# Stage boundaries of a two-layer audio tower: scatters awaited by the next stage's loads, row additions on another engine, a value table made in pieces

## The reference, cut to what matters

```python
h = signature_tokens(x) @ W.T + b                    # (32, 255, 128)
h = h + fuzzy_attention(layernorm(h))                # layer 0
h = h + experts_top1(layernorm(h))                   # 8 experts, hidden 512
h = h + relative_attention(layernorm(h))             # layer 1, 8 heads, tables of relative positions
h = h + experts_top2(layernorm(h)) + shared(...)     # 64 experts, 256 places each, hidden 64
```

## Time and profile before

| | us |
|---|---|
| median of 3 runs (lowest to highest) | 2033.37 (2031.94 to 2037.08) |
| the profiled execution, its own time | 2041.06 |
| its span in the trace | 2039.2 |
| busy in it: PE | 1724.1 |
| DVE | 1439.4 |
| ACT | 928.7 |
| POOL | 854.7 |

### The profile page before, as it was taken

How to read it: one execution, slowest core, us unless ns; L and a number is a source line. 1 busy time by engine, 2 the same in 40 slices (tenths; PEclk the granted TensorE clock), 3 DMA queues, 4 the chain that set the end, 5 groups by cost and what they waited for, 6 DMA issues and landing times. The chain is left out here.

```text
span 2039.2 us, 59053 instructions
## 1 busy us (share of the span) xinstructions
PE 1724.1 (85%) x21927; PEld 1418.4 (70%) x21927; DVE 1439.4 (71%) x3457; ACT 928.7 (46%) x2320; POOL 854.7 (42%) x1705
## 2 busy tenths in 40 slices
PE   4999999999979964994799999999999999857740
PEld 3888888888757754993577777777777777634420
DVE  6777777777668864666877888888888888644323
ACT  2211111112166722773566667666676667414320
POOL 2333333333103654666211333444444444447770
PEclk9999999999988966997799999999999999879775
DMA  8900000000040002223233333333333333345537
GB/s 300 137 0 0 0 0 0 0 0 0 1 176 11 25 28 57 71 71 109 46 62 60 70 75 70 74 70 77 73 79 74 73 73 78 86 115 158 153 94 253
DMA packets 312955, 147.80 MB, mean 72 GB/s; under 512 B 205142, under 2 KB 291572, under 8 KB 312308
## 3 DMA queue, kind: packets, MB, share of 16 engines
q1 hardware_dynamic: 300164, 118.58, 25.1%
q0 software_dynamic: 12544, 25.91, 3.9%
HBM read 72.23 MB, written 73.37 MB: 71 GB/s over the span
## 5 line engine op out<-in xcount | busy, mean ns | idle before, releaser
L1943 ACT ACTIVATE rel_e<-rel_s_ps,rel_neg_max 128x255 f32<-128x255 f32 x512 | 199.9, 478 | 42.0 <-DVE rel_neg_max L2262 41.3
L2262 DVE TENSOR_REDUCE rel_neg_max<-rel_s_ps 128x4 f32<-128x1020 f32 x128 | 156.2, 1220 | 88.4 <-PE rel_s_ps L1684 85.6
L524 PE MATMUL tok_main_ps<-tok_w_h,tok_feat_h 128*128 128x512 f32 x512 | 204.4, 399 | 1.1 <-DVE tok_feat_low L99 1.1
L524 PE MATMUL tok_main_ps<-tok_w_h,tok_feat_l 128*128 128x512 f32 x512 | 199.9, 390 | 0.0
L524 PE MATMUL tok_main_ps<-tok_w_l,tok_feat_h 128*128 128x512 f32 x512 | 199.7, 390 | 0.0
L84 POOL TENSOR_TENSOR tok_q_pre<-tok_v_q,tok_v 128x128 f32 (+1 forms) x32 | 38.8, 1213 | 305.8 <-DVE tok_q L273 291.5
L1668 PE MATMUL rel_s_ps<-rel_k_h,rel_q_head_h 128*128 128x256 f32 x512 | 156.0, 305 | 0.2 <-DVE rel_q_head_l L2233 0.2
L1705 PEld LDWEIGHTS rel_t_ps<-all_k_ident,rel_e 128*128 128x128 f32 x1024 | 109.6, 140 | 65.6 <-issue 64.5
L1705 PE MATMUL rel_t_ps<-all_k_ident,rel_e 128*128 128x128 f32 x1024 | 138.9, 278 | 11.9 <-issue 11.7
L2130 POOL DMA_INDIRECT x_slots<-rel_x,rel_at x128 | 129.9, 1015 | 38.8 <-issue 34.0
L1668 PE MATMUL rel_s_ps<-rel_k_h,rel_q_head_l 128*128 128x256 f32 x512 | 145.4, 284 | 0.0
(11 more groups left out here) (402 smaller groups left out, 4677.3 us busy)
## 6 DMA issues: line engine op xcount, KB each, us to landing
rel_q_rep<-q_rows SPq DMA_DIRECT2D x256, 64.0 KB
o_rows<-rel_rv SPq DMA_DIRECT2D x256, 64.0 KB
x_slots<-early_zeros SPq DMA_DIRECT2D x16, 520.0 KB, 6.2
exp_x<-x_slots SPq DMA_DIRECT2D x32, 260.0 KB, 3.0
y_rows<-early_zeros SPq DMA_DIRECT2D x16, 512.0 KB, 5.9
final_y<-y_rows SPq DMA_DIRECT2D x16, 512.0 KB, 10.8
exp_x<-x_slots SPq DMA_DIRECT2D x72, 65.0 KB, 1.9
q_rows<-rel_qT SPq DMA_DIRECT2D x64, 64.0 KB
```

The lines of the kernel that those rows point to most:

```text
L524: nc.tensor.matmul(main_ps[s][:, cols], feat[fk][:, s, j, :], w_p[wk][:, j, cols], start=(j == 0 and (fk, wk) == (0, 0)), stop=False)
L1943: last = nc.scalar.activation(e[u % 2][:, n, 0:L], s_ps[u % 2][:, n, 0:L], ACT.Exp, bias=neg_max[u % 2][:, n:n + 1])
L2262: nc.vector.tensor_reduce(neg_max[u % 2][:], s_ps[u % 2][:, :, 0:L], AX.X, ALU.max, negate=True)\
```

## The change

Four things are changed.

1. **Waits moved.** The semaphores of the scatters and of the padding are allocated in `build` and outlive their stages. The waits at the end of POOL's and SP's programs are gone. SP waits for the same counts in the next stage, in front of its first load: 5 semaphores and `padded` in `experts_top1`, 8 in `relative_attention`, 3 in `experts_top2`, 8 in `add_pairs`. The DRAIN and both barriers stay.
2. **Table in pieces.** In `experts_top1` DVE makes the table in 16 pieces of [128, 16 x 16], one at the end of each of steps 8 to 23, and the bias in step 24, in place of two instructions after step 71.
3. **Row additions on DVE.** DVE adds all eight chunks. Chunks 1 and 2 come behind `read_x(0)`, 3 and 4 in the head, 5, 6 and 7 in slots 1, 2 and 3 of sequence 0. Statistics: chunk 1 in the head, 2 to 5 in slots 0 to 3 of sequence 0, 6 and 7 in slots 0 and 1 of sequence 1. POOL makes the factors in two parts, chunks 1 to 3 and then 4 to 7. ACT waits for five additions ahead of the slots and for all eight in its first `rows`; DVE no longer waits. `eT` is allocated in front of `q_rep`.
4. **Order of the first loads of `experts_top2`.** SP first issues the matrices of three pairs of experts, then waits for the scatters, then loads the rows of these three, the shared matrices and the shared rows, then the rest.

```diff
@@ fuzzy_attention
-                sp.wait_ge(padded, 16 * E0)
...
-                for n in range(NB):
-                    pool.wait_ge(sent[n], 16 * CT * len(range(n, N, NB)))
@@ experts_top1
+                for j in range(NB0):
+                    sp.wait_ge(slots_sent[j], 16 * 2 * G * len(range(j, NT // (2 * G), NB0)))
+                sp.wait_ge(padded, 16 * E0)
                 for j in range(U):
                     load(j, j)
...
-                for j in range(U):
-                    pool.wait_ge(y_out[j], 16 * (ST0 // U))
...
-                def attention_tables():
-
-                    attention.wait(dve)
...
-                    for t, lo in ((1, 0), (0, 2 * P)):
-                        nc.vector.tensor_tensor(vtab[:, lo:lo + P, :], vtab[:, lo:lo + P, :],
-                                                ends[:, t:t + 1, :].to_broadcast([P, P, HD]), ALU.subtract)\
+                PIECE = 16
+                FIRST = 8
+
+                def attention_tables(n):
+
...
+                    if n == 0:
+                        attention.wait(dve)
+                        nc.vector.tensor_scalar(bq[:], bq[:], 1.0 / float(D) ** 0.5, None, ALU.mult)
+                    if 0 <= n < 2 * (P // PIECE):
+                        t, lo = ((1, 0), (0, 2 * P))[n // (P // PIECE)]
+                        rows = slice(lo + n % (P // PIECE) * PIECE, lo + (n % (P // PIECE) + 1) * PIECE)
+                        nc.vector.tensor_tensor(vtab[:, rows, :], vtab[:, rows, :],
+                                                vends[:, t:t + 1, 0:HD].to_broadcast([P, PIECE, HD]), ALU.subtract)\
                             .then_inc(table_ready, 1)
...
+                def with_tables(i, j):
+                    step(i, j)
+                    attention_tables(U * i + j - FIRST)
+
                 loaded.wait(dve)
-                run(step, 3)
-                attention_tables()
+                run(with_tables, 3)
@@ relative_attention
+                for j in range(U0):
+                    sp.wait_ge(y0_out[j], 16 * (ST0 // U0))
                 for c in range(NCH):
...
+                    if b == 0:
+                        act.wait_ge(rows_added, NCH)
...
-                    act.wait_ge(rows_added, NCH - 1)
+                    act.wait_ge(rows_added, 5)
...
-                for c in range(1, NCH):
-                    pool.wait_ge(y_in[c], 16)
-                    hc = h[:, c * CH:(c + 1) * CH, :]
-                    nc.gpsimd.tensor_tensor(hc, hc, y_at[c], ALU.add).then_inc(rows_added, 1)
-
-                def norm_rest():
+                def norm_rest(lo, hi):
...
+                    pool.wait_ge(rows_stats, hi // CH)
...
-                norm_rest()
+                norm_rest(CH, MID)
+                norm_rest(MID, NT)
...
-                for n in range(NX1):
-                    pool.wait_ge(sent[n], SENT1 * len(range(n, NC1, NX1)))
...
+                def add_rows(c):
+                    hc = h[:, c * CH:(c + 1) * CH, :]
+                    dve.wait_ge(y_in[c], 16)
+                    nc.vector.tensor_tensor(hc, hc, y_at[c], ALU.add).then_inc(rows_added, 1)
...
+                    if 2 * b == MID:
+                        dve.wait_ge(norm_ready, 2)
...
-                    if b == 0 and u in (1, 2):
-                        stats_of_rows(NCH - 3 + u)
+                    if b == 0 and u >= 1:
+                        add_rows(4 + u)
+                    if b == 0:
+                        stats_of_rows(2 + u)
+                    if b == 1 and u < 2:
+                        stats_of_rows(6 + u)
...
                     read_x(0)
-                    stats_of_rows(1)
-                    stats_of_rows(2)
+                    add_rows(1)
+                    add_rows(2)
                     keys_remainder(0, 0)
                     read_x(1)
-                    stats_of_rows(3)
+                    stats_of_rows(1)
                     read_v(0, 0)
                     queries_remainder(0, 0, range(4))
                     keys_remainder(1, 1)
-                    stats_of_rows(4)
+                    add_rows(3)
                     position_queries(0, 0)
-                    stats_of_rows(5)
+                    add_rows(4)
                     maxima(0, 0)
                     queries_remainder(1, 1, (0,))
                     read_x(2)
-                    dve.wait_ge(rows_added, NCH - 1)
@@ experts_top2
-                for j in range(U):
-                    load(0, j)
-                    if j == 1:
-                        for to, src in ((sw1_sb, sw1), (sw3_sb, sw3), (sw2_sb, sw2)):
-                            sp.dma_start(to[:], src).then_inc(sw_in, 16)
+                AHEAD = 3
+                for j in range(AHEAD):
+                    load_weights(0, j)
+                for j in range(NX1):
+                    sp.wait_ge(slots1_sent[j], 16 * CT1 * TOPK1 * len(range(j, NC1, NX1)))
+                for j in range(AHEAD):
+                    load_x(0, j)
+                for to, src in ((sw1_sb, sw1), (sw3_sb, sw3), (sw2_sb, sw2)):
+                    sp.dma_start(to[:], src).then_inc(sw_in, 16)
+                load_shared(0, 0)
+                for j in range(AHEAD, U):
+                    load_x(0, j)
+                    load_weights(0, j)
...
-                for j in range(U):
-                    pool.wait_ge(y_out[j], SENT * (N // U))
@@ add_pairs
+                for j in range(U1):
+                    sp.wait_ge(y1_out[j], 16 * (2 * CAP // P) * (E1N // 2 // U1))
                 for c in range(N):
```

More of the change, by code:

```diff
@@ L677, with fuzzy_attention @@
 CLEARS1 = (SLOTS1 + TOPK1 * NT * P) // (AGAIN * PER * P)
-def fuzzy_attention(nc, K, h, mean, rstd, stats, weights, x_slots, no_token, tables, cleared, behind):
+def fuzzy_attention(nc, K, h, mean, rstd, stats, weights, x_slots, no_token, tables, cleared, behind, sent, padded):
     ident = K["ident"]
@@ L1178, in experts_top1 @@
         x_in = [m.sem(f"x_in{j}") for j in range(U)]
-        y_out = [m.sem(f"y_out{j}") for j in range(U)]
         turned, xT_ready, w1_ready, w2_ready, hid_done, hid_a, hid_v, y_done, y_ready, tick_ready = (
@@ L1410, with relative_attention @@
 SG = 8
[L1413 removed]
+def relative_attention(nc, K, h, mean, rstd, stats, y0_rows, o_rows, q_rows, weights, x1_slots, xT_rows, placed, y0_out, sent):
     SCALE = 1.0 / float(D) ** 0.5
@@ L1424, in relative_attention @@
         q_head = [[m.sb(f"q_head{r}_{k}", [P, T // QUAD, H, QUAD], FP32R) for k in "hl"] for r in range(2)]
+        eT = [m.sb(f"eT{s}", [P, 2, NBLK // 2, P]) for s in range(2)]
         q_rep = m.sb("q_rep", [P, H, T // 2])
@@ L1428, in relative_attention @@
         neg_max = [m.sb(f"neg_max{j}", [P, UB]) for j in range(2)]
-        eT = [m.sb(f"eT{s}", [P, 2, NBLK // 2, P]) for s in range(2)]
         rv = m.sb("rv", [P, 2, NBLK // 2, QUAD * HD])
@@ L1480, in relative_attention @@
         xt_out = [m.sem(f"xt_out{j}") for j in range(2)]
-        sent = [m.sem(f"sent{n}") for n in range(NX1)]
         SENT1 = 16 * CT1 * TOPK1
@@ L2158, in norm_rest @@
+                        link(nc.gpsimd.tensor_tensor(newton_r, newton_r, var_r, ALU.mult))
+                        link(nc.gpsimd.tensor_scalar(newton_r, newton_r, -0.5, 1.5, ALU.mult, ALU.add))
+                        step = nc.gpsimd.tensor_tensor(root_r if k < 2 else rstd[:, lo:hi], root_r, newton_r,
                                                        ALU.mult)
@@ L2191, in first_rows @@
                 def first_rows():
-                    hc, first = h[:, 0:CH, :], Chain(dve, first_fac)
-                    dve.wait_ge(y_in[0], 16)
-                    nc.vector.tensor_tensor(hc, hc, y_at[0], ALU.add).then_inc(first_added, 1)
-                    dve.wait_ge(first_added, 1)
+                    first = Chain(dve, first_fac)
+                    add_rows(0)
                     stats_of_rows(0)
@@ L2510, in _, with experts_top2 @@
                 run(slot, head, tail)
-def experts_top2(nc, K, h, x1_slots, y1_rows, xT_rows, w13, w2, sw1, sw3, sw2):
+def experts_top2(nc, K, h, x1_slots, y1_rows, xT_rows, w13, w2, sw1, sw3, sw2, slots1_sent, y_out):
     ident = K["ident"]
@@ L2563, in _, with load_x @@
             def _(sp):
-                def load(i, j):
+                def load_x(i, j):
                     n = U * i + j
@@ L2578, in step @@
                         sp.wait_ge(y_out[j], SENT * i + SENT)
-                        load(i + 1, j)
+                        load_x(i + 1, j)
+                        load_weights(i + 1, j)
                         if j % 4 == 1:
@@ L2776, in _, with add_pairs @@
                 run(nc.vector, step, 1)
-def add_pairs(nc, h, y1_rows, out):
+def add_pairs(nc, h, y1_rows, out, y1_out):
     CH = 8
@@ L2971, in build @@
         cleared, cleared1, placed = m.sem("cleared"), m.sem("cleared1"), m.sem("placed")
+        slots_sent = [m.sem(f"slots_sent{j}") for j in range(NB0)]
+        padded = m.sem("padded")
```

(15 more changed lines are left out.)

63 lines of the change are left out of this document (30 added, 33 removed).

## The result

The changed kernel took 2019.84 us (median of 6 runs, 2016.61 to 2023.41), the kernel before 2034.22 beside it (6 runs). The ratio is 0.9924, with a 95% interval of 0.9908 to 0.9941: 12 to 19 us less, 15.5 at its middle. Forecast were 12.1 less, 2021.3 us, in a range of 2014 to 2031. The total was right. One term of the sum, the pieces, was 4.3 us too dear, and another, the slots, 1.2 us too cheap.

What follows compares the result with a forecast made beforehand. PE was taken as the bound inside stages, its waits at boundaries, POOL's scatters in `experts_top2`. Terms -5.3 - 3.7 + 4.3 - 11.9 + 4.0 + 0.5 = -12.1 us gave 2021.3 us, range 2014 to 2031.

Steps and rivals of the forecast that it cites:

- Waits, -5.3: Four stage boundaries: POOL's DRAIN ends earlier by the whole removed wait, less SP's waits; net 1.4, 1.3, 1.4 and 1.2 us.
- DRAINs longer by the wait removed: Sign at the stage boundaries, named in advance as showing the prediction wrong; waits of 1.5 to 1.7 us each.
- Tail, -3.7: End of `experts_top1`: without the table's two instructions the last scatter ends at about 941.0 instead of 944.74, 3.7 us less.
- Pieces, +4.3: Steps 8 to 23 of `experts_top1`: table pieces make DVE's step 2.17 us against PE's 1.90; +4.3 us, bounds 0 and 5.5.
- the pieces are hidden: `experts_top1`: a late copy starts sooner after `result` and the piece fills the gap; -16.4 us in all, 2017.0; chance 0.15.
- Pieces wait for scatters: `experts_top1`: each of 16 pieces waits up to a 0.96 us scatter; +15.4 beyond the sum, 2036.7 us; chance 0.08.
- Head, -11.9: Start of `relative_attention`: DVE, free of POOL, lets PE's first matmul start 11.9 us earlier; bounds 10 and 12.
- Slots, +4.0: Sequences 0 and 1 of `relative_attention`: added DVE work partly reaches PE, costing 4.0 us; bounds 2 and 7.
- DVE's slots cost all that they add: Slots of `relative_attention`: DVE's added work costs 10.3 us in place of 4.0, giving 2027.6 us; chance 0.12.
- First loads, +0.5: Start of `experts_top2`: matrix loads ahead of rows make the first turn 2.1 us later, first scatter +0.5; bounds -0.5 and +2.2.
- the forecast's case: Whole kernel: the summed terms hold, 12.1 us less, 2021.3 us, own range 2017 to 2026; chance 0.42.

Runs made afterwards that it cites:

- the table in one go: Changed kernel with the value table in two instructions after the last step, as before; ratio to the kernel before 0.9947, last tick to last scatter's end 5.16 us.
- holding the additions: Changed kernel with row additions on POOL and statistics in old places, POOL waiting until the first `x` is written; ratio to the kernel before 0.9950.
- the kernel with two statistics moved: Changed kernel with statistics of chunks 6 and 7 moved from slots 0 and 1 of sequence 1 to its slots 2 and 3; ratio to the kernel before 0.9939.

## Why the prediction was right in its total and wrong in a step

**Waits, -5.3: right** (-5.1 and not -5.3 mainly for the third DRAIN, and 6.0 when put back with SP's waits kept). Taking the upper bound, because a DRAIN "is work of the queue that starts when it is reached", was right. The sign that was named for a wrong step, "DRAINs longer by the wait removed", was badly chosen: the records are up to 10.5 us longer and the step is right all the same, since a queue that waits for nothing reaches its DRAIN earlier. The end against the last scatter would have been the thing to name.

**Tail, -3.7: right** (-3.5, shown by the table in one go).

**Pieces, +4.3: wrong, 0.** This is the step that failed: "Behind the copy there is no gap", "DVE's step becomes 1.86 + 0.31 = 2.17". The piece was sized right (0.34), but the 0.57 ahead of the copy were kept as if they were DVE's own time. They are the queue's register load, which the engine's work hides as soon as there is some; without them a step of DVE is 1.05 us of work, not 1.86. What came true is the rival *the pieces are hidden*, given 0.15, and for another reason than it gave: nothing starts sooner because PE is late. It should have been read from the lines of DVE's queue, whose four parts sum to the gap. *Pieces wait for scatters* (0.08) is out: steps of 1.89; it is scatters that wait, for what is left of a piece (last section).

**Head, -11.9: right** (-12.2; 14.1 when put back). The operations at 0.17 and the `x` at 0.60 came as worked out, and holding the additions shows why DVE had to take them.

**Slots, +4.0: the right mechanism, under-sized**, 5.2 with the half clock and 3.7 without. Slot by slot the split was off: slot 0 of sequence 0 with its statistics, counted as 1.4, and its slots 1 to 3, counted as 0.9, cost 1.1 together by the start of sequence 1; slots 0 and 1 of sequence 1, counted as 1.7, cost 4.1. DVE came late into sequence 1 because the idle 2.10 us ahead of the maxima of the earlier trace rows were used up, and the statistics of slot 0 added their 1.6. The window that the prediction read as sequence 0 is 0.7 us longer than it: by slot starts sequence 0 took 21.83 us with DVE busy 17.57, so DVE had some 4.3 us to spare, as was reckoned. "DVE's slots cost all that they add" (10.3) is out.

**First loads, +0.5: 0.0** in the first two traces, within a spread of 1.4 us in the others. The turn was 2.1 later as said, and that cost nothing to be seen at the first scatter.

The sum of what was measured is -5.1 - 3.5 + 0 - 12.2 + 5.2 + 0 = -15.6 us (-17.1 where the clock stays), inside the interval of -12 to -19. The forecast of -12.1 lay at its edge: the 4.3 of the pieces were too much by all of themselves, and the slots too little by 1.2. That the total came out near is therefore partly luck: the two errors work against each other, and the total can't tell the forecast's case from that of the hidden pieces, since 12.1 and 16.4 us less both lie in the interval. Only the stretches show which it was. PE's first matmul came 23.9 us earlier than 974.59, 19.4 without the 4.5 that were there ahead of the change, where 14 were forecast; the pieces are most of that too.

## What to carry to other kernels

An idle gap of an engine in front of an instruction that takes its address from a register is to be looked up in the engine's queue before it is counted as the engine's time; here 0.57 us of a 1.86 us step were free for other work. Work added to a second engine is to be costed gap by gap, by the idle time ahead of the instruction that the bound engine waits for: the same 10.3 us of added DVE work cost 5.2 us in one arrangement and 0.2 in another. A record of a DRAIN is to be read by its end, and of a wait just ahead of one nearly all was paid here.

## What the runs showed of the hardware

- **POOL's DRAIN behind scatters** ends 5.3, 5.9, 2.0 to 2.7 and 3.3 to 3.4 us behind the last scatter's end, or behind the wait for its landing where there is one, at the four boundaries in all fourteen profiles. The first, second and fourth are the same to 0.1 us with everything landed ahead of it or not; the third takes 2.0 behind the wait and 2.4 to 2.7 without. Why these lengths differ, and what it does in them, stays open; together they are some 17 us of this kernel.
- **A short wait of PE can cost twice.** Behind a wait of 2.45 us, with PE running at full clock before it, the granted clock stood at half for some 3 us and 1.6 us more were lost, in six of eight profiles that have this wait; in the other two (8.97 and 8.98 us for the slot instead of 10.57) it didn't fall. Behind another wait, of 2.03 us, in the kernel with two statistics moved, it stood at half for 3.4 us. In none of the six profiles without this wait (0.91 us in the same slot of the kernel before) did it fall in the first eight slots. Why it fell in six and not in two stays open.
- **The clock can fall without a wait of PE, too.** In every profile of the experiments, from some 1150 us on, it stands at half for 3 to 14 us (6.8 us most often), then at full for 48 to 51, over and over through `relative_attention`. Of the 53 falls between 1100 and 1850 us in four of the profiles, 47 have no wait of PE over 0.3 us in the 12 us ahead of them. In the first trace of the changed kernel it stays full there for 737 us. What makes it fall stays open.
- **A scatter waits for a DVE operation on SBUF that is already running; the other way round there is hardly a wait.** POOL beside the two pieces shown above, which began at 814.42 and 816.31:

```profile
814.47 1.23 POOL L1212 DMA_INDIRECT y_rows<-exp_y,exp_x  x1 [0.46 <-issue]
...
816.36 1.23 POOL L1212 DMA_INDIRECT y_rows<-exp_y,exp_x  x1 [0.42 <-issue]
...
818.24 0.98 POOL L1212 DMA_INDIRECT y_rows<-exp_y,exp_x  x1 [0.42 <-issue]
```

  Eight of the sixteen scatters began 0.04 to 0.10 us behind a piece. They took 1.18 to 1.24 us, and each ended 0.86 us behind the piece's end. The same 0.86 stands behind pieces of 0.68 us, for six scatters of 1.17 to 1.33, and behind the table's operations: they end at 943.89, the scatter of 2.85 us at 944.74. So a scatter is held until the running operation ends, however long that is. In the other order, or where both began within 0.03 us of each other as at 818.24, the piece took 0.42 to 0.49 us instead of 0.42, and its scatter 0.98 to 1.06. This was measured with these operations only, which have two inputs in SBUF. It cost nothing here, since a piece is short; a long operation beside the last scatter of a stage is what the tail of 3.5 us was made of.
